# Where half of a 16-row fold of down weights stands in VectorE's queue, in a two-layer audio tower

## Chip, cores, metric

One core of a Trainium2 chip. The metric is the device time in microseconds of one launch, median of several runs.

## What is computed

The reference turns 64 series of 375 samples into 256 tokens of 512 channels and runs two layers over them: a quantised attention and a mixture of 16 experts (top 2), then a grouped attention and a feed-forward network (FFN) between two Hadamard transforms. The change touches the last part only:

```python
x = fwht(x * SU_ug) / SCALE                               # over 512
x_up = x @ W_up.T * (Wscale_ug[:INTER] * SCALE)
x_gate = x @ W_gate.T * (Wscale_ug[INTER:] * SCALE)
x = jax.nn.silu(x_gate) * x_up
x = fwht(x * SU_dp) / SCALE                               # over 2048
x = x @ W_down.T * (Wscale_dp * SCALE)
```

## The kernel before

Each engine has one queue of instructions in an order written out by hand; engines wait for each other by semaphores. Tokens stand in two tiles of 128. Matrix products are made in float32 precision from three products of rounded operands: every weight and activation is split into a high half (a cast, ScalarE, `*_high`) and a low half (value minus high half, VectorE, `*_low`).

**The stages.** After embedding and the first attention (to about 60 us) come the experts in 8 pairs (`for p in range(2, PAIRS)`, about 72 to 171 us), the second attention (to about 208 us), and the FFN: 2048 inner channels in FC = 16 chunks of 128.

**The FFN loop.** For chunk f, TensorE (`ffn_gu(f)`) makes gate and up products, 24 matmuls, in banks j = f % 2. It waits for the chunk's weights (`fw_ready`, from `f_low(f)`) and for the gating of chunk f - 2. ScalarE applies silu to the gate, then casts the weights of chunk f + 2 (`f_high`, two buffers `f_hi`, free when chunk f has ended). VectorE multiplies (the gating product, L1685, `s_fh`), then makes the low half of chunk f + 2 (`f_low`, L1551, `s_f_lo`). Every four chunks VectorE makes the part of the second Hadamard transform that goes across chunks (`within_pairs` L1654 and L1655, `across_pairs` L1664, `u_low` L1670), and from chunk 7 on TensorE follows each chunk by one step of the down product (`down(f - 7)`, L687 to L689), which needs a row of split down weights (`wd_high` L649, `wd_low` L1675, four buffers) and a half of u (`u_ready`).

**The fold.** The rest of the 2048-wide Hadamard transform is put into the down weights, which stand in SBUF as 16 rows of 128x512. Across partitions TensorE turns each row by a 128x128 Hadamard matrix (`turn(i)`, copied back by ScalarE, semaphore `turned`). Across rows VectorE folds them by sums and differences of row pairs: rows 0, 1, 4, 5, 8, 9, 12, 13 in pieces 0 to 3, the others in pieces 4 to 7. A piece is `fold_even`, `fold_odd`, `fold_sums` (two 128x1024 operations each) or `fold_rest` (three). Row turning and folding may come in either order, but a fold must find its rows all turned or none. Scratch is tile `s_fold` in the expert stage (its memory belongs to the experts' tiles) and `s_u` for piece 7. Before, piece 0 stands in pair 1, pieces 1 to 6 in pairs 2 to 7, each behind `hidden_low(3 * p)`, and piece 7 just ahead of the FFN. The first increment of `fold_done`, behind the experts, lets TensorE turn the remaining rows; the second, behind piece 7, lets ScalarE start on `wd_high(0)`. `wd_of(f)` lists which rows are split in iteration f, on ScalarE and VectorE alike.

Of the kernel before, what the change touches and what calls it, by code (L numbers as in the profile page):

```python
# [25 lines left out]
ALU = mybir.AluOpType  # L26
# [19 lines left out]
PAIRS = E // 2  # L46
MOE_F32 = 4 * KC * GU + 2 * 3 * C
I = 2048
FC = I // P
# [26 lines left out]
def tower(nc, patches, tok_w, tok_b, att_w, router, moe_gu, moe_dn, l1_w, vec_cols, ws_dp, ffn_w,  # L76
          down_w, consts, out):
    with ExitStack() as ctx:
# [3 lines left out]
        def sem(name):  # L82
            return ctx.enter_context(nc.semaphore(name))
# [82 lines left out]
        dn_done, fold_done = sem("dn_done"), sem("fold_done")  # L166
# [7 lines left out]
        turn_done, turned, hd_read = sem("turn_done"), sem("turned"), sem("hd_read")  # L174
# [15 lines left out]
        A, B, L, M = {}, {}, {}, {}  # L190
# [78 lines left out]
        def ffn_chunk_raw(f):  # L269
            return ffn_raw[:, f * FCH:(f + 1) * FCH].rearrange("p (k n) -> p k n", k=KC)  # L270
# [25 lines left out]
        def half_of(ap, i):  # L296

            return ap[:, 2 * i:2 * i + 2, :]
# [5 lines left out]
        def wd_of(f):  # L304

            if f < 8:
                return (f,) if f < 4 else ()
            q = f // 4 - 1
            return ((), (4 * q,), (4 * q + 1,), (4 * q + 2,) if f == FC - 1 else (4 * q + 2, 4 * q + 3))[f % 4]

# [4 lines left out]
        def heads(ap):  # L315
            return ap.rearrange("p (h d) -> p h d", h=H)
# [11 lines left out]
        def tb(t, n):  # L328
            return bank[4 * t + n]
# [101 lines left out]
        def _(act):  # L431
# [210 lines left out]
            act.copy(h[:, 1, :], tb(1, 3)[:]).then_inc(h_kept, 1)  # L642

            def wd_high(c):
                if c == 0:
                    act.wait_ge(fold_done, 2)
                if c >= 4:
                    act.wait_ge(down_done, c - 3)
                act.copy(wd_hi[:, c % 4, :], down_raw[:, c, :]).then_inc(wdh_ready, 1)  # L649
# [434 lines left out]
        def _(dve):  # L1084
            o = Order(dve, dve_ord)
# [207 lines left out]
            for t in range(TILES):  # L1293
                a, a8, summed = am3[:, :, t], k16, heads(tb(t, 3)[:])
# [46 lines left out]
            def main_low(e):  # L1341
                dve.wait_ge(guh_ready, e + 1)
                dve.tensor_tensor(B["gu_lo"][e % 2][:], main_of(e), B["gu_hi"][e % 2][:].bitcast(F32), ALU.subtract  # L1343
                                  ).then_inc(gu_ready, 1)

            def rest_low(p):
                dve.wait_ge(resth_ready, 2 * p + 2)
                for j in range(2):
                    for up in range(2):
                        last = dve.tensor_tensor(rest_part("rest_lo", 2 * p + j, up), rest_of(2 * p + j, up),  # L1350
                                                 rest_part("rest_hi", 2 * p + j, up).bitcast(F32), ALU.subtract)
                last.then_inc(rest_ready, 1)

            def dn_low(p):
                dve.wait_ge(dnh_ready, p + 1)
                dve.tensor_tensor(B["dn_lo"][:], moe_dn_raw(p), B["dn_hi"][:].bitcast(F32), ALU.subtract
                                  ).then_inc(dn_ready, 1)
# [48 lines left out]
            def gate_up(n):  # L1406

                dve.wait_ge(silu_done, n + 1)
                dve.wait_ge(up_done, n + 1)
                if n >= 3:  # L1410
                    dve.wait_ge(cb_done, n + 1)
                if n >= 4:
                    dve.wait_ge(h_ready, n - 3)
                dve.tensor_tensor(B["hm"][n % 4][:], up_bank(n)[:, 0:TOK], B["silu"][n % 2][:], ALU.mult
                                  ).then_inc(mul_done, 1)

            def weighted(n):

                if n < 3:
                    dve.wait_ge(cb_done, max(n + 1, 2))  # L1420
                dve.wait_ge(mul_done, n + 1)
                dve.tensor_tensor(B["hm"][n % 4][:], cb_of(n), B["hm"][n % 4][:], ALU.mult).then_inc(h_raw, 1)  # L1422

            def hidden_low(n):

                p, part = n // 3, n % 3
                dve.wait_ge(h_hi, n + 1)
                dve.tensor_tensor(B["ht_lo"][p % 2][:, part, :], B["hm"][n % 4][:],
                                  B["ht_hi"][p % 2][:, part, :].bitcast(F32), ALU.subtract).then_inc(h_ready, 1)

            def w1_low(k):

                dve.wait_ge(w1h_ready, k + 1)
                dve.tensor_tensor(w1_lo[:, k, :], qkv1_raw[:, k, :], w1_hi[:, k, :].bitcast(F32), ALU.subtract
                                  ).then_inc(w1_ready, 1)

            fold = B["fold"][:]

            def fold_of(g):

                return (down_raw[:, 2 * (g // 4) + 4 * i:2 * (g // 4) + 4 * i + 2, :] for i in range(4))

            def fold_even(g):

                s0, s1, s2, s3 = fold_of(g)
                if g == 0:
                    dve.wait_ge(ld_down, 16)
                    dve.wait_ge(turned, TURNS_FIRST)
                o.settle()
                o.mark(dve.tensor_tensor(fold, s0, s2, ALU.add))  # L1450
                o.mark(dve.tensor_tensor(s2, s0, s2, ALU.subtract))

            def fold_odd(g):
# [6 lines left out]
            def fold_sums(g):  # L1460

                s0, s1, s2, s3 = fold_of(g)
                o.settle()
                o.mark(dve.tensor_tensor(s1, fold, s0, ALU.subtract))
                o.mark(dve.tensor_tensor(s0, fold, s0, ALU.add))

            def fold_rest(g):

                s0, s1, s2, s3 = fold_of(g)
                spare = fold if g < PAIRS - 1 else M["u"][:].rearrange("p (a b) n -> p a (b n)", a=2)  # L1470
                o.settle()
                o.mark(dve.tensor_tensor(spare, s2, s3, ALU.add))
                o.mark(dve.tensor_tensor(s3, s2, s3, ALU.subtract))
                o.settle()
                o.mark(dve.tensor_copy(s2, spare))

            def fold_piece(g):

                (fold_even, fold_odd, fold_sums, fold_rest)[g % 4](g)
# [28 lines left out]
            for p in range(2, PAIRS):  # L1508
                rest_low(p)
                hidden_low(3 * p - 1)  # L1510
                gate_up(3 * p)
                weighted(3 * p)
                if p + 1 < PAIRS:
                    main_low(2 * p + 2)
                hidden_low(3 * p)
                fold_piece(p - 1)
                if p < 2 + KC:
                    w1_low(p - 2)
                else:
                    i = p - 2 - KC  # L1520
                    dve.wait_ge(o1h_ready, i + 1)
                    dve.tensor_tensor(half_of(L["o_lo"], i), half_of(o1_raw, i), half_of(L["o_hi"], i).bitcast(F32),
                                      ALU.subtract).then_inc(o1_ready, 1)
                dn_low(p)
                gate_up(3 * p + 1)
                weighted(3 * p + 1)
                if p + 1 < PAIRS:
                    main_low(2 * p + 3)
                hidden_low(3 * p + 1)
                gate_up(3 * p + 2)  # L1530
                weighted(3 * p + 2)
# [17 lines left out]
            def f_low(f):  # L1549
                dve.wait_ge(fwh_ready, f + 1)  # L1550
                dve.tensor_tensor(M["w_lo"][f % 2][:], ffn_chunk_raw(f), M["w_hi"][f % 2][:].bitcast(F32), ALU.subtract  # L1551
                                  ).then_inc(fw_ready, 1)
# [85 lines left out]
            xt_low(8)  # L1638
            normalised(3, 1, M["xn"], tb(1, 3)[:]).then_inc(xn_ready, 1)
            xt_low(9)  # L1640
            dve.wait_ge(turned, FC)
            fold_piece(PAIRS - 1)
            o.settle()
            dve.sem_inc(fold_done, 1)
            for n in range(2):
                dve.wait_ge(xfh_ready, n + 1)
                dve.scalar_tensor_tensor(M["xf_lo"][:, 2 * n:2 * n + 2, :], tb(n, 2)[:].rearrange("p (k n) -> p k n", k=2),
# [25 lines left out]
            def wd_low(c):  # L1673
                dve.wait_ge(wdh_ready, c + 1)
                dve.tensor_tensor(wd_lo[:, c % 4, :], down_raw[:, c, :], wd_hi[:, c % 4, :].bitcast(F32),  # L1675
                                  ALU.subtract).then_inc(wd_ready, 1)

            o.settle()
            for f in range(FC):
                j = f % 2  # L1680
                dve.wait_ge(fsilu, f + 1)
                dve.wait_ge(fu_done, f + 1)
                if f >= 8:
                    dve.wait_ge(hd_read, f // 4 - 1)
                dve.scalar_tensor_tensor(M["h"][f // 4 % 2][:, f % 4, :], tb(j, 1)[:, 0:TOK], wsu_c[:, f:f + 1], M["silu"][j][:],  # L1685
                                         ALU.mult, ALU.mult).then_inc(fglu, 1)
                if f + 2 < FC:
                    f_low(f + 2)
                if f >= 4 and f % 4 < 3:
                    (within_pairs, across_pairs, u_low)[f % 4](f // 4 - 1)  # L1690
                for c in wd_of(f):
                    wd_low(c)
# [85 lines left out]
```

## Time and profile before

| | |
|---|---|
| median of 3 runs | 289.25 us (289.17 to 290.2) |
| the profiled execution: its time, its span | 288.17 us, 286.3 us |
| TensorE matmul busy | 269.5 us (94%), 1704 instructions |
| TensorE weight load busy | 224.8 us (79%) |
| VectorE busy | 232.0 us (81%), 424 instructions |
| ScalarE busy | 149.0 us (52%), 235 instructions |
| GpSimd busy | 9.7 us (3%) |
| DMA | 40.45 MB, mean 141 GB/s |

The span runs from the first to the last instruction; the time holds something around it, too. Busy time of TensorE is modelled at its ends (matmuls are pipelined), so a full 100% can hide short waits. In the rows PE is TensorE, PEld its weight load, DVE VectorE, ACT ScalarE, POOL GpSimd, SP the queue that issues DMAs; L1685 is line 1685 of the kernel. A row of the timeline gives start and length in us, the line, what is written and read, and in brackets the idle time ahead of it with the engine that ended it. "x2" is two instructions in one row. One instruction starts before the row ahead of it has run out: lengths overlap by about 0.1 us on VectorE, so queues are costed from start to start.

### The profile page before, as it was taken

Reading aid. Unit: us, or ns where it says so; the run is one execution under the profiler, and the core shown is the slowest. Engines: PE = TensorE matmul, PEld = TensorE weight load, DVE = VectorE, ACT = ScalarE, POOL = GpSimd, SP = SyncE. Lnnn points to the kernel's source line nnn. Section 1 sums busy time; section 2 is a strip of 40 time slices with the busy share of each in tenths; the row PEclk is TensorE's granted clock in tenths of the full one; section 3 lists DMA queues with packets and bytes.
Section 4 is the critical chain, followed back from the end, with each engine's and each line's share of the span. In section 5 each row is a group of like instructions: output and inputs, shape, how many; then the busy total and the mean of one; then the engine's idle time right before and its main releaser. Section 6 shows DMA issues by size and latency. Waiting matters only on the chain. (4 is left out here: it accounts for less than half of the span.)

```text
span 286.3 us, 4458 instructions
## 1 busy us (share of the span) xinstructions
PE 269.5 (94%) x1704; PEld 224.8 (79%) x1707; DVE 232.0 (81%) x424; ACT 149.0 (52%) x235; POOL 9.7 (3%) x29
## 2 busy tenths in 40 slices
PE   8689569999999999999999999999999999999993
PEld 3445344859999899999989886875689999999962
DVE  1959999797997999899999856699777895777783
ACT  2997770144754665646566434344347672663530
POOL 0200000010000000000000004100100000000000
PEclk9979979999999999999999999999999999999998
DMA  6950399945080836446510068077000000000003
GB/s 248 416 228 0 93 396 400 413 203 193 30 310 23 290 149 222 161 173 215 185 40 1 2 224 362 2 282 304 0 2 0 2 1 2 0 0 2 1 0 73
DMA packets 6566, 40.45 MB, mean 141 GB/s; under 512 B 1169, under 2 KB 1425, under 8 KB 5266
## 3 DMA queue, kind: packets, MB, share of 16 engines
q1 hardware_dynamic: 6546, 40.18, 37.3%
q8 instruction: 13, 0.21, 0.3%
q14 instruction: 7, 0.06, 0.1%
HBM read 39.13 MB, written 0.52 MB: 138 GB/s over the span
## 5 line engine op out<-in xcount | busy, mean ns | idle before, releaser
L902 PE MATMUL bank<-s_xt_hi,s_gu_hi 128*128 128x256 f32 x120 | 34.0, 283 | 0.0
L903 PE MATMUL bank<-s_xt_lo,s_gu_hi 128*128 128x256 f32 x120 | 33.9, 283 | 0.0
L904 PE MATMUL bank<-s_xt_hi,s_gu_lo 128*128 128x256 f32 x120 | 33.9, 282 | 0.0
L1036 PE MATMUL bank<-s_xf_hi,s_f_lo 128*128 128x256 f32 x128 | 31.1, 281 | 0.0
L1036 PE MATMUL bank<-s_xf_hi,s_f_hi 128*128 128x256 f32 x128 | 31.1, 281 | 0.0
L1551 DVE TENSOR_TENSOR s_f_lo<-s_ffn_raw,s_f_hi 128x1024 fp32r<-128x1024 f32 x16 | 19.6, 1225 | 6.6 <-ACT s_f_hi L605 6.5
L1036 PEld LDWEIGHTS bank<-s_xf_hi,s_f_hi 128*128 128x128 f32 x128 | 24.1, 188 | 0.4
L1036 PEld LDWEIGHTS bank<-s_xf_hi,s_f_lo 128*128 128x128 f32 x128 | 24.1, 188 | 0.3
L902 PEld LDWEIGHTS bank<-s_xt_hi,s_gu_hi 128*128 128x128 f32 x120 | 23.0, 191 | 0.2
L903 PEld LDWEIGHTS bank<-s_xt_lo,s_gu_hi 128*128 128x128 f32 x120 | 22.9, 191 | 0.2
L904 PEld LDWEIGHTS bank<-s_xt_hi,s_gu_lo 128*128 128x128 f32 x120 | 22.9, 191 | 0.0
L471 ACT CAST s_gu_hi<-s_moe_raw 128x1024 fp32r<-128x1024 f32 x16 | 16.7, 1047 | 10.1 <-PE bank L904 10.0
L661 ACT ACTIVATE s_fs<-bank,s_cols 128x256 f32<-128x256 f32 x16 | 7.6, 474 | 25.3 <-PE bank L1053 25.3
L687 PE MATMUL bank<-s_dn_hi,s_ht_hi 128*128 128x512 f32 x48 | 18.9, 394 | 0.0
L689 PE MATMUL bank<-s_dn_hi,s_ht_lo 128*128 128x512 f32 x48 | 18.8, 391 | 0.0
L688 PE MATMUL bank<-s_dn_lo,s_ht_hi 128*128 128x512 f32 x48 | 18.7, 389 | 0.0
L1343 DVE TENSOR_TENSOR s_gu_lo<-s_moe_raw,s_gu_hi 128x1024 fp32r<-128x1024 f32 x15 | 18.3, 1217 | 0.1
L904 PE MATMUL bank<-s_xt_hi,s_rest_lo 128*128 128x256 f32 x64 | 18.1, 282 | 0.0
L903 PE MATMUL bank<-s_xt_lo,s_rest_hi 128*128 128x256 f32 x64 | 18.1, 282 | 0.0
L902 PE MATMUL bank<-s_xt_hi,s_rest_hi 128*128 128x256 f32 x64 | 18.1, 282 | 0.0
L1053 PE MATMUL bank<-s_xf_lo,s_f_hi 128*128 128x256 f32 x128 | 17.8, 281 | 0.0
L531 ACT CAST s_ht_hi<-s_hm 128x256 fp32r<-128x256 f32 x24 | 9.6, 406 | 15.4 <-DVE s_hm L1422 15.2
(249 smaller groups left out, 679.4 us busy)
## 6 DMA issues: line engine op xcount, KB each, us to landing
s_moe_raw<-moe_gu SPq DMA_DIRECT2D x16, 768.0 KB, 5.9
s_ffn_raw<-ffn_w SPq DMA_DIRECT2D x4, 2048.0 KB, 9.9
s_moe_raw<-moe_dn SPq DMA_DIRECT2D x8, 768.0 KB, 4.5
s_big_raw<-att_w SPq DMA_DIRECT2D x4, 1024.0 KB, 8.2
s_big_raw<-down_w SPq DMA_DIRECT2D x1, 4096.0 KB, 20.0
s_l_raw<-l_w SPq DMA_DIRECT2D x1, 2560.0 KB, 25.6
out<-s_h SPq DMA_DIRECT2D x4, 128.0 KB, 2.3
s_tok_w<-tok_w SPq DMA_DIRECT2D x1, 256.0 KB, 2.9
```

The lines of the kernel that those rows point to most:

```text
L471: act.copy(B["gu_hi"][e % 2][:], main_of(e)).then_inc(guh_ready, 1)
L531: act.copy(B["ht_hi"][p % 2][:, part, :], B["hm"][n % 4][:]).then_inc(h_hi, 1)
L687: pe.matmul(dst, x_hi, w_hi, start=first, stop=False)
L688: pe.matmul(dst, x_hi, w_lo, start=False, stop=False)
L689: return pe.matmul(dst, x_lo, w_hi, start=False, stop=last)
L902: pe.matmul(dst, w_hi, xt_hi[:, k, :], start=(k == 0), stop=False)
L903: pe.matmul(dst, w_hi, xt_lo[:, k, :], start=False, stop=False)
L904: last = pe.matmul(dst, w_lo, xt_hi[:, k, :], start=False, stop=(k == KC - 1))
L1036: pe.matmul(tb(j, n)[:, 0:TOK], M[w][j][:, k, n * P:(n + 1) * P], M["xf_hi"][:, k, :], start=(w == "w_hi" and k == 0), stop=False)
L1053: last = pe.matmul(tb(j, n)[:, 0:TOK], M["w_hi"][j][:, k, n * P:(n + 1) * P], M["xf_lo"][:, k, :], start=False, stop=(k == KC - 1))
L1343: dve.tensor_tensor(B["gu_lo"][e % 2][:], main_of(e), B["gu_hi"][e % 2][:].bitcast(F32), ALU.subtract).then_inc(gu_ready, 1)
L1551: dve.tensor_tensor(M["w_lo"][f % 2][:], ffn_chunk_raw(f), M["w_hi"][f % 2][:].bitcast(F32), ALU.subtract).then_inc(fw_ready, 1)
```

## The change

Pieces 4 to 7 of the fold leave their places (4 to 6 in expert pairs 5 to 7, 7 ahead of the FFN) and stand in iterations 0 to 3 of the FFN loop on VectorE, each behind `f_low(f + 2)`. The wait for all rows to be turned moves to iteration 0, the second increment of `fold_done` to iteration 4. All four pieces use `s_u` as scratch. Rows 0 and 1 of the down weights are split in iterations 0 and 1 as before; rows 2 and 3 move from iterations 2 and 3 to 5 and 6. ScalarE's wait for the second `fold_done` stands ahead of `wd_high(2)` in place of `wd_high(0)`. No operation is added or removed in sum.

```diff
--- before.py
+++ after.py
@@ -304,7 +304,7 @@
         def wd_of(f):
 
             if f < 8:
-                return (f,) if f < 4 else ()
+                return (f,) if f < 2 else (f - 3,) if 4 < f < 7 else ()
             q = f // 4 - 1
             return ((), (4 * q,), (4 * q + 1,), (4 * q + 2,) if f == FC - 1 else (4 * q + 2, 4 * q + 3))[f % 4]
 
@@ -642,7 +642,7 @@
             act.copy(h[:, 1, :], tb(1, 3)[:]).then_inc(h_kept, 1)
 
             def wd_high(c):
-                if c == 0:
+                if c == 2:
                     act.wait_ge(fold_done, 2)
                 if c >= 4:
                     act.wait_ge(down_done, c - 3)
@@ -1440,6 +1440,10 @@
 
                 return (down_raw[:, 2 * (g // 4) + 4 * i:2 * (g // 4) + 4 * i + 2, :] for i in range(4))
 
+            def fold_to(g):
+
+                return fold if g < PAIRS // 2 else M["u"][:].rearrange("p (a b) n -> p a (b n)", a=2)
+
             def fold_even(g):
 
                 s0, s1, s2, s3 = fold_of(g)
@@ -1447,7 +1451,7 @@
                     dve.wait_ge(ld_down, 16)
                     dve.wait_ge(turned, TURNS_FIRST)
                 o.settle()
-                o.mark(dve.tensor_tensor(fold, s0, s2, ALU.add))
+                o.mark(dve.tensor_tensor(fold_to(g), s0, s2, ALU.add))
                 o.mark(dve.tensor_tensor(s2, s0, s2, ALU.subtract))
 
             def fold_odd(g):
@@ -1461,13 +1465,13 @@
 
                 s0, s1, s2, s3 = fold_of(g)
                 o.settle()
-                o.mark(dve.tensor_tensor(s1, fold, s0, ALU.subtract))
-                o.mark(dve.tensor_tensor(s0, fold, s0, ALU.add))
+                o.mark(dve.tensor_tensor(s1, fold_to(g), s0, ALU.subtract))
+                o.mark(dve.tensor_tensor(s0, fold_to(g), s0, ALU.add))
 
             def fold_rest(g):
 
                 s0, s1, s2, s3 = fold_of(g)
-                spare = fold if g < PAIRS - 1 else M["u"][:].rearrange("p (a b) n -> p a (b n)", a=2)
+                spare = fold_to(g)
                 o.settle()
                 o.mark(dve.tensor_tensor(spare, s2, s3, ALU.add))
                 o.mark(dve.tensor_tensor(s3, s2, s3, ALU.subtract))
@@ -1513,7 +1517,8 @@
                 if p + 1 < PAIRS:
                     main_low(2 * p + 2)
                 hidden_low(3 * p)
-                fold_piece(p - 1)
+                if p <= PAIRS // 2:
+                    fold_piece(p - 1)
                 if p < 2 + KC:
                     w1_low(p - 2)
                 else:
@@ -1638,10 +1643,6 @@
             xt_low(8)
             normalised(3, 1, M["xn"], tb(1, 3)[:]).then_inc(xn_ready, 1)
             xt_low(9)
-            dve.wait_ge(turned, FC)
-            fold_piece(PAIRS - 1)
-            o.settle()
-            dve.sem_inc(fold_done, 1)
             for n in range(2):
                 dve.wait_ge(xfh_ready, n + 1)
                 dve.scalar_tensor_tensor(M["xf_lo"][:, 2 * n:2 * n + 2, :], tb(n, 2)[:].rearrange("p (k n) -> p k n", k=2),
@@ -1686,6 +1687,13 @@
                                          ALU.mult, ALU.mult).then_inc(fglu, 1)
                 if f + 2 < FC:
                     f_low(f + 2)
+                if f < PAIRS // 2:
+                    if f == 0:
+                        dve.wait_ge(turned, FC)
+                    fold_piece(PAIRS // 2 + f)
+                if f == PAIRS // 2:
+                    o.settle()
+                    dve.sem_inc(fold_done, 1)
                 if f >= 4 and f % 4 < 3:
                     (within_pairs, across_pairs, u_low)[f % 4](f // 4 - 1)
                 for c in wd_of(f):
```

## Rows read from the trace of the kernel before

**Rows 1.** Cores: span, mean granted TensorE clock.
```profile
core 0: 286.3 us, clock 0.983
```

**Rows 2.** Windows: stage, its length, busy us (x instructions) per engine, PEclk, DMA, GB/s.
```profile
72.00:171.00 99.00, 99.00 (x708) 93.19 (x706) 90.33 (x151) 56.03 (x105) 0.00 (x0) 1.00 0.40 142
...
212.30:275.00 62.70, 62.39 (x458) 58.98 (x456) 47.62 (x68) 34.89 (x54) 0.00 (x0) 1.00 0.00 1
...
235.60:275.00 39.40, 39.40 (x264) 36.17 (x264) 28.94 (x43) 19.28 (x31) 0.00 (x0) 1.00 0.00 1
```

**Rows 3.** Waits, 72 to 171 us: engine, line waited for: total us, times, longest.
```profile
PEld bank L687 <- DVE s_ht_lo L1428: 0.4, 1, 0.4
```

**Rows 4.** Timeline, VectorE, experts: start us, length us, instruction [idle before, releaser].
```profile
135.28 1.22 DVE L1450 TENSOR_TENSOR s_fold<-s_big_raw 128x1024 f32<-128x1024 f32 x1
136.42 1.22 DVE L1451 TENSOR_TENSOR s_big_raw<-s_big_raw 128x1024 f32<-128x1024 f32 x1
```

**Rows 5.** Timeline, VectorE, just ahead of the FFN.
```profile
210.30 1.22 DVE L1473 TENSOR_TENSOR s_big_raw<-s_big_raw 128x1024 f32<-128x1024 f32 x1
211.56 0.69 DVE L1475 COPY s_big_raw<-s_u 128x1024 f32<-128x1024 f32 x1
212.39 1.47 DVE L1647 SCALAR_TENSOR_TENSOR s_xf_lo<-bank,s_xf_hi 128x512 fp32r<-128x512 f32 x2
```

**Rows 6.** Timeline, VectorE, first FFN chunks.
```profile
215.50 0.48 DVE L1685 SCALAR_TENSOR_TENSOR s_fh<-bank,s_cols,s_fs 128x256 f32<-128x256 f32 x1 [1.64 <-ACT s_fs L661]
...
216.48 1.22 DVE L1551 TENSOR_TENSOR s_f_lo<-s_ffn_raw,s_f_hi 128x1024 fp32r<-128x1024 f32 x1 [0.49 <-ACT s_f_hi L605]
...
217.62 0.69 DVE L1675 TENSOR_TENSOR s_wd_lo<-s_big_raw,s_wd_hi 128x512 fp32r<-128x512 f32 x1
...
219.33 1.23 DVE L1551 TENSOR_TENSOR s_f_lo<-s_ffn_raw,s_f_hi 128x1024 fp32r<-128x1024 f32 x1 [0.52 <-ACT s_f_hi L605]
...
229.01 0.68 DVE L1654 TENSOR_TENSOR s_half_rotated<-s_fh 128x512 f32<-128x512 f32 x1
...
229.61 0.68 DVE L1655 TENSOR_TENSOR s_half_rotated<-s_fh 128x512 f32<-128x512 f32 x1
...
234.77 1.29 DVE L1670 TENSOR_TENSOR s_u_lo<-s_u,s_u_hi 128x512 fp32r<-128x512 f32 x2
...
235.97 0.48 DVE L1685 SCALAR_TENSOR_TENSOR s_fh<-bank,s_cols,s_fs 128x256 f32<-128x256 f32 x1
...
236.41 1.23 DVE L1551 TENSOR_TENSOR s_f_lo<-s_ffn_raw,s_f_hi 128x1024 fp32r<-128x1024 f32 x1
```

**Rows 7.** Timeline, TensorE, first FFN chunks.
```profile
214.25 0.28 PE L1053 MATMUL bank<-s_xf_lo,s_f_hi 128*128 128x256 f32 x1
...
218.04 0.28 PE L1036 MATMUL bank<-s_xf_hi,s_f_hi 128*128 128x256 f32 x1
...
220.89 0.28 PE L1036 MATMUL bank<-s_xf_hi,s_f_hi 128*128 128x256 f32 x1
...
232.28 0.28 PE L1036 MATMUL bank<-s_xf_hi,s_f_hi 128*128 128x256 f32 x1
...
235.60 0.47 PE L687 MATMUL bank<-s_wd_hi,s_u_hi 128*128 128x512 f32 x1 [0.31 <-DVE s_u_lo L1670]
```

**Rows 8.** Timeline, ScalarE, casts of the chunks' weights.
```profile
215.39 1.05 ACT L605 CAST s_f_hi<-s_ffn_raw 128x1024 fp32r<-128x1024 f32 x1
...
235.33 1.05 ACT L605 CAST s_f_hi<-s_ffn_raw 128x1024 fp32r<-128x1024 f32 x1
```

**Rows 9.** Timeline, VectorE, later chunk.
```profile
240.17 0.48 DVE L1685 SCALAR_TENSOR_TENSOR s_fh<-bank,s_cols,s_fs 128x256 f32<-128x256 f32 x1 [2.53 <-ACT s_fs L661]
```

**Rows 10.** Windows: stretches with idle TensorE, PEclk behind POOL.
```profile
10.00:14.00 4.00, 2.09 (x19) 1.48 (x17) 3.65 (x13) 3.88 (x4) 1.57 (x6) 0.98 1.01 426
...
14.00:17.30 3.30, 3.08 (x10) 1.49 (x11) 2.22 (x9) 3.30 (x2) 0.00 (x0) 0.50 1.04 402
...
198.00:202.00 4.00, 2.82 (x19) 2.34 (x18) 3.73 (x8) 1.30 (x3) 0.55 (x1) 1.00 0.09 37
```

## Prediction

> **What bounds the kernel now.** I read the span and clock first, then the busy time by stage, then the waits, then the order of single instructions around the change. The profiled execution has a span of 286.3 us at a granted clock of 0.983 [rows 1]; its own device time was 288.17 us, against a median of 289.25 us over the three runs. In the expert stage (72 to 171 us) TensorE is busy all 99.00 us and VectorE 90.33 us; in the FFN (212.3 to 275 us) TensorE is busy 62.39 of 62.70 us and VectorE 47.62 [rows 2]. Busy TensorE time is modelled, so I also looked at waits: in the expert stage the view of waits has no entry for TensorE's matmuls, and only one of 0.4 us for its weight load [rows 3]. So TensorE sets both stages, and VectorE, though 91% busy in the first, is just in time.
>
> The decisive thing is how much "just in time" is in the FFN. TensorE starts chunk 2 at 218.04 and chunk 3 at 220.89, so one chunk is 2.85 us of matmuls [rows 7]. For chunk 3 it needs the low half of that chunk's weights, which VectorE makes from 219.33 for 1.23 us, that is until 220.56 [rows 6]. The cover is 0.33 us. It is not a buffer that could run ahead: w_lo has two buffers, so the low half of chunk f + 2 can only be made after chunk f has ended, and VectorE makes it in iteration f, behind the gating product of chunk f (line 1685).
>
> **What the change removes.** Pieces 4, 5 and 6 leave the expert stage: two 128x1024 operations each, 1.22 us long, started 1.14 us apart [rows 4], so 3 x 2.28 = 6.84 us of VectorE. TensorE waits for nothing there [rows 3], so this gives 0 on the path; the price if I am wrong is the first rival. Piece 7 leaves the stretch ahead of the FFN: three operations, the last two at 210.30 and 211.56, and the next work at 212.39 [rows 5]. Behind it stand the two operations that make xf_lo (1.47 us together, to 213.86), first read by TensorE at 214.25 [rows 7]. TensorE works through the chunk's high products until then, and only ScalarE's xf_hi gates those. Gain 0. The waits for `turned` and `fold_done` move too, with no instruction of another queue passed: no DMA is issued by any moved step, and SP and POOL wait for none of them.
>
> **What it adds, step by step.** Iterations 0 to 3 get one piece each, placed between the low half of chunk f + 2 and the next gating product. My prices are starts to starts in the same queue: gating product 0.44 (235.97 to 236.41), low half 1.14 (216.48 to 217.62) and 1.23 until it is ready, a 128x512 operation 0.60 (229.01 to 229.61) [rows 6], a piece of two operations 2.28 [rows 4], piece 7 1.14 + 1.26 + 0.60 = 3.00, where 210.30 to 211.56 is the 1.26 with the wait between them [rows 5]. A matmul starts 0.04 us after the operation that frees it (an estimate, from the ScalarE cast ended 216.44 and the VectorE operation at 216.48 behind it [rows 6, 8]).
>
> Iteration 0: product at 215.50 and low half of chunk 2 at 216.48 as before. Chunk 2 starts at 218.04, unmoved. Piece 4 runs 217.62 to 219.90, wd_low(0) to 220.50.
> Iteration 1: product 220.50, low half of chunk 3 at 220.94, ready for TensorE 222.20. TensorE wanted it at 220.89: **it stands 1.31 us**. Piece 5 runs 222.08 to 224.36, wd_low(1) to 224.96.
> Iteration 2: low half of chunk 4 at 225.40, usable 226.66; chunk 3 ended 222.20 + 2.85 = 225.05: **1.61 us**. Piece 6 runs 226.54 to 228.82; there is no wd_low here any more.
> Iteration 3: low half of chunk 5 at 229.26, usable 230.52; chunk 4 ended 229.51: **1.01 us**. Piece 7 runs 230.40 to 233.40.
> Iteration 4: low half of chunk 6 at 233.84, usable 235.10; chunk 5 ended 233.37: **1.73 us**. Then fold_done and within_pairs, 234.98 to 236.18.
> Iteration 5: low half of chunk 7 at 236.62, usable 237.88, in time (chunk 6 ends 237.95). across_pairs to 238.96, the moved wd_low(2) to 239.56.
> Iteration 6: product, low half of chunk 8 at 240.00, then u_low(0) at 241.14, first half ready 241.83. TensorE ends chunk 7 at 240.80 and needs it for down(0). Before, that half was ready at 234.77 + 0.69 = 235.46 (the row shows both halves; 0.69 is one 128x512 operation, as at 217.62) and down(0) started at 235.60, 0.47 us after the end of chunk 7 at 232.28 + 2.85 = 235.13 [rows 6, 7]. With the same 0.14 us it now starts at 241.97.
>
> **Sum.** 241.97 - 235.60 = 6.37 us later. The stalls say the same: 1.31 + 1.61 + 1.01 + 1.73 = 5.66, and 1.17 against 0.47 at down(0) gives 0.70 more, together 6.36. The added VectorE work is 9.84 us, less 0.60 for wd_low(3), which ends up behind u_low(0); 2.87 us of the rest go into idle time that VectorE had in these iterations (0.49 and 0.52 us waits for ScalarE's cast are two of them [rows 6]).
>
> **What hides, and what does not come back.** From down(0) on a chunk and its down step take TensorE 4.2 us, and VectorE has waits such as the 2.53 us at 240.17 [rows 9], so it catches up within two iterations. TensorE does not: from 235.6 to 275 us it was busy 39.40 of 39.40 us before [rows 2], so its lateness is carried to the end at full size. wd_high(2) on ScalarE now waits for the second fold_done, given near 235.0; behind it stand the activation of chunk 6 (wanted at 237.6) and the later casts. ScalarE comes to that wait about 234.65, behind a cast of 1.05 us like the one at 235.33 [rows 8], so it waits some 0.3 us and nobody behind it is held: 0. The bounds of what no row shows: the wait at the head of a piece may cost up to the 0.12 us by which 1.26 is over 1.14, four times, and the other pitches up to 0.1 us in a few places; downwards nothing excludes 0.1 us less. So +6.2 to +7.1, and I take 6.4. Span 286.3 + 6.4 = 292.7 us; from the profiled execution's own time 288.17 + 6.4 = 294.6; from the median **289.25 + 6.4 = 295.6 us**.
>
> **Rivals.** (1) *The experts were paced by VectorE after all*: the 91% busy VectorE sets TensorE's pitch in a way that the waits don't show. Then up to 6.84 us come back and the change ends at 289.25 + 6.37 - 6.84 = 288.8 us, no slower. It decides as soon as one matmul there waited for a low half; rows 3 speak against it. 4%, half of that beyond 0.5% faster.
> (2) *The pieces fit into VectorE's idle time*: the FFN has 62.70 - 47.62 = 15.08 us of it [rows 2], more than 9.84, so by sums nothing is late: 289.25 us. It would need the low halves to be ready early, and the cover of 0.33 us says they are not. 4%. The Trainium skill (Perfetto Trace Analysis, Optimization Strategy) says that with several regimes "performance may be improved by interleaving those regimes", and takes the most occupied engine of each for its limit; by that rule a move of work from the 91% stretch to the 76% stretch is this rival or better. The cover in rows 6 and 7 speaks against it.
> (3) *The clock falls as well*. TensorE would now stand 5.66 of the 18 us from 217 to 235. Its clock was granted at 0.98 in a stretch with 2.09 of 4 us busy and was 0.50 right behind it, while a stretch with 2.82 of 4 us kept 1.00 [rows 10]. Chunks 3 to 6 have it at work 2.85 us in each 3.9 to 4.6, nearer to the latter. One fall for 3.3 us at 0.50 loses 1.6 us of matmul time, part of it in the shadow of VectorE: up to 297.2 us. 11%. The Trainium skill (TensorE: Matmul & The Clock Gate, What's actually happening) calls the throttled state the default that activity releases, which leaves room for it.
>
> **How the numbers follow.** Forecast 81%, rivals 4, 4 and 11%. The range goes from the profiled execution's base, 288.17 + 6.2 = 294.4 less 0.1 for spread, to one fall of the clock, 297.2 and some spread, 297.5. About 0.5% is what a measurement of this kernel can tell from no change. Faster by over 0.5%: 2%; within: 6%; slower: 92%.
>
> **What would show it.** Right: in the profile after, VectorE's pieces stand between two low halves of 1.2 us from 217 to 234 us; TensorE waits for s_f_lo four times, 1.0 to 1.7 us each, and at down(0) for s_u_lo near 1.2 us; the start of the FFN is unmoved at 212.3; the stretch behind down(0) has its old length. Wrong: if the FFN starts earlier, rival 1 is at work; if TensorE shows no wait for s_f_lo, rival 2; if rows after 220 us show a clock under 1.00, rival 3. The sum is off if TensorE takes longer to start again after a wait than 0.04 us.

## The result, and the profile after

The changed kernel takes 294.81 us (four runs, 293.37 to 296.2) against 289.21 us for the kernel before (four runs, 287.33 to 290.2): a ratio of 1.0201, 95% interval 1.0129 to 1.0273, so it is slower by 5.6 us. The profiled execution has a span of 292.8 us at a granted clock of 0.983, where before had 286.3 us at the same clock [rows 1].

The view of windows of the kernel after, to be read as [rows 2]: the expert stage in the same window, the FFN cut at its own start and at down(0), so those two windows are not those of before (start:end, length, busy time of TensorE, its weight load, VectorE, ScalarE, GpSimd, granted clock, DMA share, GB/s):

```profile
72.00:171.00 99.00, 99.00 (x709) 93.58 (x708) 83.73 (x147) 56.14 (x106) 0.00 (x0) 1.00 0.39 139
...
212.70:242.10 29.40, 24.10 (x195) 23.10 (x194) 26.34 (x33) 15.83 (x24) 0.00 (x0) 1.00 0.00 1
242.10:281.30 39.20, 39.20 (x263) 36.14 (x264) 29.29 (x44) 18.66 (x31) 0.00 (x0) 1.00 0.00 1
```

In the expert stage VectorE fell from 90.33 to 83.73 us busy, by the pieces that left, and TensorE is busy all 99.00 us as before: nothing was gained there. The loss is in the second row, the first chunks, where TensorE is busy 24.10 of 29.40 us while VectorE is busy 26.34. Behind down(0) TensorE is full again. What TensorE waited for in these stretches (total us, times, longest):

```profile
PE bank L1036 <- DVE s_f_lo L1556: 4.5, 4, 1.4
...
PE bank L687 <- DVE s_u_lo L1671: 0.8, 1, 0.8
```

The first line is new; the second had 0.31 us before [rows 7]. These are the places where TensorE stands, in its timeline of after; they answer to [rows 7]:

```profile
214.67 1.11 PE L1053 MATMUL bank<-s_xf_lo,s_f_hi 128*128 128x256 f32 x8
...
222.59 0.38 PE L1036 MATMUL bank<-s_xf_hi,s_f_hi 128*128 128x256 f32 x1 [1.11 <-DVE s_f_lo L1556]
...
226.99 0.39 PE L1036 MATMUL bank<-s_xf_hi,s_f_hi 128*128 128x256 f32 x1 [1.29 <-DVE s_f_lo L1556]
...
230.78 0.39 PE L1036 MATMUL bank<-s_xf_hi,s_f_hi 128*128 128x256 f32 x1 [0.69 <-DVE s_f_lo L1556]
...
235.31 0.38 PE L1036 MATMUL bank<-s_xf_hi,s_f_hi 128*128 128x256 f32 x1 [1.41 <-DVE s_f_lo L1556]
...
242.06 0.47 PE L687 MATMUL bank<-s_wd_hi,s_u_hi 128*128 128x512 f32 x1 [0.80 <-DVE s_u_lo L1671]
```

The bracket counts from the modelled end of the last matmul, so it is shorter than the loss. From start to start, with 2.85 us for a chunk, chunk 3 loses 222.59 - (215.62 + 2 x 2.85) = 1.27 us (chunk 1 began at 215.62, 0.95 behind the first low product of chunk 0), chunks 4, 5 and 6 lose 1.55, 0.94 and 1.68, and down(0) 1.05.

The VectorE queue around the first of these, to be held against [rows 6]:

```profile
220.92 0.48 DVE L1686 SCALAR_TENSOR_TENSOR s_fh<-bank,s_cols,s_fs 128x256 f32<-128x256 f32 x1
221.32 1.21 DVE L1556 TENSOR_TENSOR s_f_lo<-s_ffn_raw,s_f_hi 128x1024 fp32r<-128x1024 f32 x1
222.45 1.22 DVE L1461 TENSOR_TENSOR s_big_raw<-s_big_raw 128x1024 f32<-128x1024 f32 x1
223.58 1.22 DVE L1462 TENSOR_TENSOR s_big_raw<-s_big_raw 128x1024 f32<-128x1024 f32 x1
224.72 0.68 DVE L1676 TENSOR_TENSOR s_wd_lo<-s_big_raw,s_wd_hi 128x512 fp32r<-128x512 f32 x1
225.32 0.48 DVE L1686 SCALAR_TENSOR_TENSOR s_fh<-bank,s_cols,s_fs 128x256 f32<-128x256 f32 x1
```

No bracket stands in it: VectorE never waits. One iteration takes it 225.32 - 220.92 = 4.40 us, TensorE's chunk takes 2.85. The same holds for the whole stretch: behind the low half of chunk 2, started at 216.91, VectorE's rows have no bracket up to u_low(0) at 241.23 (L1671). So u_low(0) comes when the work ahead of it in this queue is done.

**A measure that resolves this.** The medians scatter by more than 1 us, so the experiments are also read by one distance in each trace: from the first low product of chunk 0 (L1053, s_xf_lo) to the first matmul of down(0) (L687). Before it is 235.60 - 214.25 = 21.35 us, after 242.06 - 214.67 = 27.39: 6.04 us more. The distance from there to the end of the span is 50.7 us in both. Inserted lines shift the line numbers of the experiments a little.

The ratios below compare with the kernel before as it ran beside each group of experiments: median 288.82 us for the first four, 288.65 us for the next four. The diffs are against the changed kernel where nothing else is said, and show the part that matters; "..." marks what is left out.

### The profile page after: what moved, and what is told of

It is laid out like the page before. It is cut to its first block and busy times, and to the rows that moved or that the text cites. A ratio compares the mean times of both kernels' runs of the same rounds, so it can differ in the third digit from the quotient of the medians.

```text
span 292.8 us, 4461 instructions
## 1 busy us (share of the span) xinstructions
PE 272.0 (93%) x1707; PEld 226.8 (77%) x1707; DVE 231.1 (79%) x424; ACT 148.9 (51%) x235; POOL 10.0 (3%) x29
## 5 line engine op out<-in xcount | busy, mean ns | idle before, releaser
L1356 DVE TENSOR_TENSOR s_dn_lo<-s_moe_raw,s_dn_hi 128x1536 fp32r<-128x1536 f32 x8 | 14.0, 1755 | 7.2 <-ACT s_dn_hi L518 7.2
L687 PE MATMUL bank<-s_dn_hi,s_ht_hi 128*128 128x512 f32 x48 | 18.9, 394 | 0.0
L1053 PE MATMUL bank<-s_xf_lo,s_f_hi 128*128 128x256 f32 x128 | 17.8, 281 | 0.0
```

Source lines behind the costliest of these rows:

```text
L687: pe.matmul(dst, x_hi, w_hi, start=first, stop=False)
L1053: last = pe.matmul(tb(j, n)[:, 0:TOK], M["w_hi"][j][:, k, n * P:(n + 1) * P], M["xf_lo"][:, k, :], start=False, stop=(k == KC - 1))
```

## Experiments

**The loop without the pieces.** The kernel leaves out the nine operations of pieces 4 to 7 altogether. Theory: these operations in VectorE's queue are the cost. Main rival: the experts were paced by VectorE.

```diff
                 if f + 2 < FC:
                     f_low(f + 2)
-                if f < PAIRS // 2:
-                    if f == 0:
-                        dve.wait_ge(turned, FC)
-                    fold_piece(PAIRS // 2 + f)
+                if f == 0:
+                    dve.wait_ge(turned, FC)
```

> The changed kernel with the operations of pieces 4 to 7 left out everywhere (so the fold of half of the down weights is missing from the result); the moved waits, the moved fold_done and the moved splits of rows 2 and 3 stay. Measure: the distance from the first low product of chunk 0 (L1053) to the first matmul of down(0) (L687), 21.35 us in the kernel before (214.25 to 235.60) and 27.39 in the changed one (214.67 to 242.06). Theory (the VectorE queue of the first chunks): the nine operations are the cost; what is left is wd_low(2) ahead of u_low(0), 0.5 us, so 21.85 us and a median near 289.7. Rival 1 (the experts were paced by VectorE and gained up to 6.84 us that the FFN hides): the expert stage is shorter by some us and the time falls to 283 to 287. Rival 'the moved splits are free': 21.35 us.

Measured: 289.02 us, ratio 1.0024 (0.9991 to 1.0056); distance 236.83 - 215.05 = 21.78 us.

```profile
236.83 0.47 PE L687 MATMUL bank<-s_wd_hi,s_u_hi 128*128 128x512 f32 x1 [0.73 <-DVE s_u_lo L1671]
```

The four waits for s_f_lo are gone and so is the loss, but for 0.43 us at down(0): the bracket is 0.73 us in place of 0.31 in [rows 7]. With all of pieces 4 to 7 out of the experts and out of the stretch ahead of the FFN, nothing came back: from the first expert matmul to the last of the experts it took 106.93 us, against 106.22 before. Rival 1 falls.

**Rows 2 and 3 split later.** Does the second part of the change cost anything by itself?

```diff
-                return (f,) if f < 2 else (f - 3,) if 4 < f < 7 else ()
+                return (f,) if f < 2 else (2,) if f == 7 else ()
+            if f == 8:
+                return (3,)
```

> The changed kernel with rows 2 and 3 split in iterations 7 and 8 in place of 5 and 6. Theory: every 0.60 us ahead of u_low(0) on VectorE is paid by TensorE at down(0), so the distance falls from 27.39 to 26.8 us and the time by 0.6 us to near 294.2. Rival: down(0) is late by the late chunks only and the split costs nothing: 27.39 us.

Measured: 294.12 us, ratio 1.0185 (1.0124 to 1.0246); distance 239.82 - 212.92 = 26.90 us, 0.49 less. The row at down(0) has a wait of 0.30 us in place of 0.80; the four before it are 1.11, 1.29, 0.68 and 1.38 us, as in the changed kernel. So about 0.5 of the 6.04 us is the split of row 2 standing ahead of u_low(0), and it costs about the same with the pieces as without them (0.43 us in the run above).

**Piece 7 alone, in one block.** A dose of three operations instead of nine, all in iteration 3. Rows 2 and 3 are split in iterations 7 and 8, as in the run above.

```diff
-                if p <= PAIRS // 2:
-                    fold_piece(p - 1)
+                fold_piece(p - 1)
...
-                if f < PAIRS // 2:
-                    if f == 0:
-                        dve.wait_ge(turned, FC)
-                    fold_piece(PAIRS // 2 + f)
+                if f == PAIRS // 2 - 1:
+                    dve.wait_ge(turned, FC)
+                    fold_piece(PAIRS - 1)
```

> Pieces 4 to 6 back in the expert stage, only piece 7 (three operations, 3.00 us) in the FFN loop, all in iteration 3; rows 2 and 3 split in iterations 7 and 8. Theory: VectorE has 3.00 us more between two low halves, of which some 1.6 us fall into idle time and cover, so TensorE stands 1.4 us once, at chunk 6, and the distance is 22.8 us, the time near 290.7. Rival 2 (added work below the sum of VectorE's idle time is hidden): 21.35 us. Rival 'a price per operation added': 3/9 of 6.04 = 2.0 us.

Measured: 290.18 us, ratio 1.0054 (1.002 to 1.0088); distance 237.86 - 214.97 = 22.89 us, 1.54 more than before.

```profile
231.56 0.39 PE L1038 MATMUL bank<-s_xf_hi,s_f_hi 128*128 128x256 f32 x1 [1.23 <-DVE s_f_lo L1557]
```

One wait for a low half, at chunk 6, behind the 3.00 us piece. Against the kernel before, the two splits of 0.60 us each have also left the stretch ahead of u_low(0), so 1.54 us is the price of 3.00 us in one block beside 1.20 us less of other work.

**Piece 7 alone, one operation in each of three iterations.** The same three operations, but cut apart and over iterations 1, 2 and 3. The chunks are not the same, though the expectation below says so: the block stood in iteration 3 alone, so the run changes grain and place together. The diff is against the run with the block.

```diff
-                if f == PAIRS // 2 - 1:
+                if f == 1:
                     dve.wait_ge(turned, FC)
-                    fold_piece(PAIRS - 1)
+                if 1 <= f < 4:
+                    s0, s1, s2, s3 = fold_of(PAIRS - 1)
+                    spare = fold_to(PAIRS - 1)
+                    if f == 1:
+                        o.mark(dve.tensor_tensor(spare, s2, s3, ALU.add))
+                    elif f == 2:
+                        o.mark(dve.tensor_tensor(s3, s2, s3, ALU.subtract))
+                    else:
+                        o.settle()
+                        o.mark(dve.tensor_copy(s2, spare))
```

> As the run with piece 7 in one block, but its three operations one each in iterations 1, 2 and 3. Same work in the same chunks. Theory: one 1.14 us operation beside wd_low fits nearly into the 0.5 us wait for the cast, the place of the removed split and the 0.33 us cover, so TensorE stands 0.2 us or less, the distance is 21.5 us and the time near 289.4. Rival 'a price per operation added': the same as the block, 2.0 us.

Measured: 288.6 us, ratio 1.0 (0.9959 to 1.0042); distance 237.01 - 215.43 = 21.58 us.

```profile
223.98 1.11 PE L1055 MATMUL bank<-s_xf_lo,s_f_hi 128*128 128x256 f32 x8
225.06 0.38 PE L1038 MATMUL bank<-s_xf_hi,s_f_hi 128*128 128x256 f32 x1
...
237.01 0.47 PE L689 MATMUL bank<-s_wd_hi,s_u_hi 128*128 128x512 f32 x1 [0.31 <-DVE s_u_lo L1672]
```

No bracket for s_f_lo is left, and the one at down(0) is that of [rows 7]. The starts show a small stall all the same: chunk 4 begins at 225.06, right behind its low half (223.79 + 1.21 = 225.00 in VectorE's rows), where 223.98 + 0.95 = 224.93 would have been full pace, and the low products of chunk 4 start 3.07 us behind those of chunk 3 in place of 2.85. That is the 0.23 us. So a price per operation is out: the same 3.00 us cost 1.54 us as a block in iteration 3 and 0.23 us as single operations over three iterations, both beside the same 1.20 us less of splits. A mere sum over the stage is out too, by the block. Which part of the difference is the grain and which the place was not separated.

**Piece 4 ahead of the FFN, in the idle time there.**

```diff
             xt_low(9)
+            dve.wait_ge(turned, FC)
+            fold_piece(PAIRS // 2)
...
-                if f < PAIRS // 2:
-                    if f == 0:
-                        dve.wait_ge(turned, FC)
+                if 0 < f < PAIRS // 2:
                     fold_piece(PAIRS // 2 + f)
```

> The changed kernel with piece 4 where piece 7 stood before (ahead of the FFN, between the last xt_low and the two operations of xf_lo), pieces 5 to 7 in iterations 1 to 3. Theory: ahead of the FFN VectorE has 5.1 us of idle time in the changed kernel (2.23, 1.21 and 1.64 us), so piece 4 is free there, TensorE no longer stands at chunk 3, and the distance from the first low product of chunk 0 to down(0) falls from 27.39 to 25.9 us, the time to near 293.2. Rival (the four stalls have a price each for starting again, whatever the amount of work): three stalls of about 1.1 us left, 26.3 us. Rival 2 (sums): 21.35 us.

Measured: 293.1 us, ratio 1.0158 (1.0109 to 1.0207); distance 240.61 - 214.77 = 25.84 us, 1.55 less than the changed kernel. The rows show waits of 1.11, 0.68 and 1.41 us at chunks 4 to 6. The stall at chunk 3 is gone and the first one has moved to chunk 4: part of the excess of the first piece in the loop is covered wherever it comes, and 2.28 us of work taken out give back 1.55. The idle time ahead of the FFN hid the piece (the stretch from the experts to the first low product stayed at 41.33 us), as it hid piece 7 before.

**Four buffers.** The prediction gave the double buffer as the reason why the low halves can't be early. This run gives them more room: the high halves get four buffers, the low halves go to ffn_lo, a tile over the memory of the raw weights with a place for each chunk, and those of chunks 2 and 3 are made ahead of the loop.

```diff
-            M["w_hi"] = [sb(f"f_hi{j}", [P, KC, 2 * P], F32R, s) for j in range(2)]
-            M["w_lo"] = [sb(f"f_lo{j}", [P, KC, 2 * P], F32R, s) for j in range(2)]
+            M["w_hi"] = [sb(f"f_hi{j}", [P, KC, 2 * P], F32R, s) for j in range(4)]
+            M["w_lo"] = [ffn_lo[:, f * FCH:(f + 1) * FCH].rearrange("p (k n) -> p k n", k=KC) for f in range(FC)]
...
-                if f + 2 < FC:
-                    f_low(f + 2)
+                if f + 4 < FC:
+                    f_low(f + 4)
```

> The changed kernel with four buffers for the high halves of the FFN weights and the low halves written over the raw weights (16 places): low halves of chunks 2 and 3 are made ahead of the loop, and iteration f makes that of chunk f + 4. The work in each iteration is the same, the cover of a chunk grows from 0.33 us by two chunks. Rival 'the cover alone is what failed' (as the prediction put it: the low halves cannot be made early): the stalls go and the distance falls to 22 us or less, the time to 289.5. Theory (VectorE's total work ahead of u_low(0)): iterations 0 to 6 hold as many operations as before, so down(0) is no earlier, the distance stays within 0.3 us of 27.4 us and the time near 294.8; the stall at chunk 3 is gone, the lateness of chunk 6 is near 4.4 us in place of 5.6, and the rest moves to down(0).

Measured: 295.49 us, ratio 1.0248 (1.0195 to 1.03); distance 243.10 - 215.66 = 27.44 us, the same as the changed kernel's 27.39. TensorE's timeline:

```profile
226.98 0.36 PE L1039 MATMUL bank<-s_xf_hi,s_f_hi 128*128 128x256 f32 x1 [1.30 <-DVE s_fh L1692]
...
235.31 0.36 PE L1039 MATMUL bank<-s_xf_hi,s_f_hi 128*128 128x256 f32 x1 [1.47 <-DVE s_fh L1692]
...
243.10 0.47 PE L690 MATMUL bank<-s_wd_hi,s_u_hi 128*128 128x512 f32 x1 [1.90 <-DVE s_u_lo L1677]
```

The releaser has changed: no longer the low half but s_fh, the gating product of chunk f - 2, which frees the PSUM banks and stands in the same queue behind the same pieces; and u_low(0) is no earlier (it starts 242.27 - 215.66 = 26.61 us behind the first low product, 26.56 in the changed kernel), so down(0) takes what the chunks gained. Chunk 6 starts 19.65 us behind the first low product, against 20.64 in the changed kernel and 15.18 before, 4.47 us late as expected, and the wait at down(0) is 1.90 us in place of 0.80.

**Low halves of chunks 2 and 3 ahead of the loop, none in iterations 0 and 1.** The same buffers, less lead, but less work in the queue ahead of u_low(0). The diff is against the run with four buffers; the casts on ScalarE are changed alike.

```diff
-                if f + 4 < FC:
-                    f_low(f + 4)
+                if 2 <= f < FC - 2:
+                    f_low(f + 2)
```

> As the run with four buffers, low halves of chunks 2 and 3 made ahead of the loop, but iterations 0 and 1 then make none, and iteration f from 2 on makes that of chunk f + 2 as in the changed kernel. So 2.28 us of VectorE work leave the stretch ahead of u_low(0) and nothing else differs. Theory: the distance falls by 2.3 to 2.9 us, to 24.5 to 25.1, the time to near 292. Rival 'cover': with less lead than the run with four buffers it is no faster than that run.

Measured: 292.63 us, ratio 1.0148 (1.0097 to 1.02); distance 241.03 - 216.50 = 24.53 us, 2.91 less than with four buffers and the full lead. The waits left:

```profile
234.28 0.39 PE L1039 MATMUL bank<-s_xf_hi,s_f_hi 128*128 128x256 f32 x1 [1.42 <-DVE s_ffn_lo L1559]
...
241.03 0.47 PE L690 MATMUL bank<-s_wd_hi,s_u_hi 128*128 128x512 f32 x1 [0.84 <-DVE s_u_lo L1677]
```

Two brackets at the chunks in place of four (the other one is 0.71 us, at chunk 5), and the releaser is the low half again, since in this run it has lost its lead by chunk 5. Here the buffers paid: without them the low halves of chunks 2 and 3 could not be made ahead of the loop.

**u_low(0) first, in the kernel before.** The one wait that the kernel before had in the FFN loop.

```diff
+                if f == 6:
+                    u_low(0)
                 if f + 2 < FC:
                     f_low(f + 2)
-                if f >= 4 and f % 4 < 3:
+                if f >= 4 and f % 4 < 3 and f != 6:
```

(and the same on ScalarE with u_high.)

> The kernel before, with u_high(0) and u_low(0) of iteration 6 ahead of the cast and low half of chunk 8. Theory: down(0) waits for u_low(0) by 0.31 us in the row and starts 0.47 us after the end of chunk 7, while the low half of chunk 8 is needed 1.4 us later, so the distance falls from 21.35 to 20.9 us and the time by 0.4 us to near 288.8, at the limit of what can be told. Rival: the cast of chunk 8 gets late by 0.9 us and gives the 0.4 us back: 21.35 us to chunk 8's start.

Measured: 287.87 us, ratio 0.9982 (0.9944 to 1.0021); distance 235.21 - 214.33 = 20.88 us.

```profile
235.21 0.39 PE L689 MATMUL bank<-s_wd_hi,s_u_hi 128*128 128x512 f32 x1
```

The wait is gone and the trace gives 0.47 us for it. In device time that lies inside the interval, so a faster kernel is shown in the trace alone, and not by its time. The rival falls: the first low product of chunk 8 comes 238.50 - 214.33 = 24.17 us behind that of chunk 0, against 238.97 - 214.25 = 24.72 before, so the later cast gave nothing back.

**Both kernels once more**, to tell a kernel's own time from an execution's.

> The kernel before, profiled once more. Question: from trace to trace the stretch ahead of the experts ended between 65.4 and 68.6 us and the experts took 106.2 to 106.9 us, whatever the kernel. If these differences belong to the execution, the same kernel shows them too, while its distance from the first low product of chunk 0 to down(0) stays at 21.35 us within 0.1. If they belong to the kernels, all three repeat (66.7, 106.2, 21.35).

> The changed kernel, profiled once more, for the same question: distance 27.39 us within 0.1 in both cases; the start of the experts and their length repeat (66.6, 106.7) only if they belong to the kernel.

Measured, in us: first expert matmul at, from there to the last one of the experts' down product, from there to the first low product of chunk 0, from there to down(0).

| | start | experts | second attention | distance |
|---|---|---|---|---|
| before | 66.72 | 106.22 | 41.31 | 21.35 |
| before again | 67.12 | 106.62 | 41.33 | 21.36 |
| changed | 66.62 | 106.72 | 41.33 | 27.39 |
| changed again | 67.79 | 106.71 | 41.31 | 27.40 |

The start and the length of the experts differ between executions of the same kernel; the last two columns repeat to 0.02 us. From down(0) to the end of the span it took 50.70, 50.77, 50.74 and 50.99 us.

## Why the prediction was right, point by point

- *Nothing is gained in the experts.* Right. Shown by the loop without the pieces, and by 99.00 us of busy TensorE with 6.60 us less of VectorE. The 0.50 us by which the experts took longer in the first trace of after belongs to the execution: the kernel before took 106.62 us in its other trace. The windows from 66 to 72 us, before and then after, show a difference in the granted clock there, 1.00 against 0.84:

```profile
66.00:72.00 6.00, 5.91 (x51) 5.71 (x50) 4.24 (x14) 3.77 (x6) 0.00 (x0) 1.00 0.69 244
...
66.00:72.00 6.00, 6.00 (x45) 6.00 (x45) 3.56 (x12) 3.15 (x6) 0.00 (x0) 0.84 0.76 262
```

- *Nothing is gained ahead of the FFN.* Right: 41.31 and 41.33 us.
- *The walk through VectorE's queue.* Right in every stall: 1.31, 1.61, 1.01, 1.73 and 1.17 us foreseen, 1.27, 1.55, 0.94, 1.68 and 1.05 measured. The sum of 6.37 us came out at 6.04. The term that was a little too large is the pitch of the gating product. 0.44 us was read from 235.97 to 236.41, but the operation at 236.41 followed ScalarE's cast, which ended at 235.33 + 1.05 = 236.38 [rows 8], so a wait too short for a bracket was in it; in the full queue the pitch is 221.32 - 220.92 = 0.40, six times over. The 128x1024 operations follow each other by 1.13 in place of 1.14 us. That the span of 292.8 us met the forecast of 292.7 is luck: the 0.50 us that the experts took longer made up for the sum. The time of 294.81 lies 0.8 us under the forecast of 295.6.
- *The 0.04 us from release to matmul.* A little too small, without effect: the low half that ended at 221.32 + 1.21 = 222.53 let the matmul start at 222.59, 0.06 us later.
- *ScalarE's wait for the second fold_done.* The 0.3 us foreseen don't show. wd_high(2) starts at 234.89 without a bracket, 0.95 us behind the start of the cast ahead of it (233.94). That nobody behind it is held was right.
- *The lateness is not given back.* Right: 50.70 and 50.74 us from down(0) to the end of the span.
- *The moved split costs part of it.* It was in the sum, and the two runs on it give 0.43 and 0.49 us.
- *The double buffer as the reason.* As a statement on the code it holds. As the reason for the loss it is incomplete, though this did not change the number. More buffers and more lead, with the same work in each iteration, left the distance at 27.44 us. What binds is the work that VectorE has to do ahead of u_low(0), and the gating product in the same queue; the cover of 0.33 us only sets at which chunk the first stall shows. The buffers are worth something where they let work leave the loop: with two low halves made ahead of it the distance was 2.91 us shorter than with four buffers alone, at less lead.
- *Rival 2 (the idle time of the stage holds it).* It fell: the FFN had 15.08 us of idle VectorE and still lost 6.04 us. Its grain of truth is in the pair on piece 7: as single operations over three iterations the same work did fit, but for 0.23 us, and nothing was gained by it either (ratio 1.0). The Trainium skill (Perfetto Trace Analysis, Optimization Strategy) proposes interleaving for kernels in which the most contended engine changes over time. In this kernel TensorE is the busiest engine of both stages, by its matmuls and by its weight load [rows 2], so the prediction applied that sentence to a case that it does not describe, and no run here tests it.
- *Rival 3 (the clock).* It did not happen: 1.00 in the stretch of 212.70 to 242.10, with TensorE busy 24.10 of 29.40 us.

## What to carry to other kernels

Where an engine feeds another chunk by chunk, price a moved piece of work against the slack of one chunk, not against the idle share of the stage, and walk through the feeding queue from start to start up to the next point where the fed engine has slack. Work on an engine that is 91% busy is not worth moving while the engine that sets the pace shows no wait for it. If it has to be moved, put it in as single operations over several iterations, each where the queue waits anyway. This was shown for three operations; for all nine it was not run, and since VectorE showed no wait from 216.91 us to u_low(0), another order of the same work would not bring u_low(0) forward (argued, not shown). More buffers alone don't help while all releases come out of the same queue; they help where they let work leave it.

## What the runs showed that was not expected

- The start of the program, up to the first expert matmul, took from 65.36 us (in the run with rows 2 and 3 later) to 68.56 us (in the run with the low halves ahead), and 66.62 and 67.79 us for one and the same kernel, while the second attention took 41.31 to 41.37 us in all traces. Most of the scatter of this kernel's time is thus older than the changed code, and distances inside a trace resolve what medians don't. The records show what it goes with: over the 38 executions of the kernel before beside the experiments, those with a granted clock of 0.994 over the span took 286.65 to 287.91 us, those with 0.975 or 0.976 took 289.9 to 290.65 us. In the traces the clock stands at 1.00 from 172 to 243 us; it differs ahead of that, in the first 66 us between 0.92 and 0.97. The experts took 106.21 and 106.22 us in the two traces with 1.00 from 66 to 72 us, and 106.45 to 106.93 us in the ten with 0.72 to 0.89. What makes the clock differ between executions of one kernel is open, and not all of the start is the clock: the latest start, 68.56 us, came at 0.95.
- VectorE in a full queue starts the next operation 1.13 us behind a 128x1024 one that its row gives as 1.22 us long, 0.60 behind a 128x512 one (0.68) and 0.40 behind the gating product of 128x256 from PSUM (0.48).
- Standing up to 1.68 us between bursts of 2.85 us, four times in a row, left TensorE's granted clock at 1.00.
